# Graph layers: a ring of two groups of eight gather buffers, rows as three bf16 parts

## The reference

```python
x = x + gnn(layernorm(x), edge_index, edge_attr, ...)      # x: 6250 nodes x 256
x = x + ffn(layernorm(x), ...)                             # shared and top-2-of-8 routed experts, 256 -> 1024 -> 256

# gnn: h = x; five layers of
edge_fea = concat([edge_attr[:, 3:] @ ew1[l], edge_attr[:, 0:3] @ ew2[l]])
msg  = norm[:, None] * (h[row] + edge_fea)                 # 106250 edges; norm = dinv[row] * dinv[col]
agg  = segment_sum(msg, col)
h    = relu(concat([h, agg]) @ mlp_w[l] + mlp_b[l])
h    = batchnorm(h) * bn_g[l] + bn_b[l]                    # over the nodes; relu after it but in the last layer
```

## Time and profile before

| | us |
|---|---|
| timed runs, median | 7337.11 |
| profiled execution, first to last instruction (its span) | 8853.9 |
| preparation, to the first gather | 252 |
| gather loop of layer 0 / of layers 1 to 4 | 1480 / 1368 to 1377 |
| each of four changes of layer | 51 to 52 |
| feed-forward part | 1426 |

### The profile page before, as it was taken

How to read it: one execution, slowest core, us unless ns; L and a number is a source line. 1 busy time by engine, 2 the same in 40 slices (tenths; PEclk the granted TensorE clock), 3 DMA queues, 4 the chain that set the end, 5 groups by cost and what they waited for, 6 DMA issues and landing times. The chain is left out here.

```text
span 8853.9 us, 124916 instructions
## 1 busy us (share of the span) xinstructions
PE 6519.7 (74%) x24773; PEld 4847.4 (55%) x24774; DVE 2838.4 (32%) x9215; ACT 1624.7 (18%) x6511; POOL 4159.8 (47%) x4391
## 2 busy tenths in 40 slices
PE   3666676677777777777777777777777776789998
PEld 2444454545555545555555555555555554568886
DVE  9444444433233333333233332323222224210002
ACT  5111111111111111111121111111111112222222
POOL 0455555455555545555545555554555553210003
PEclk9777777777777777777777777777777777899999
DMA  1322222232222232222232222223222222311112
GB/s 48 90 75 73 73 73 74 76 95 79 78 78 80 78 97 80 81 77 79 79 93 83 79 77 79 81 78 96 79 79 77 79 80 74 120 51 54 54 46 85
DMA packets 316995, 687.46 MB, mean 78 GB/s; under 512 B 82064, under 2 KB 171203, under 8 KB 316819
## 3 DMA queue, kind: packets, MB, share of 16 engines
q0 software_dynamic: 214352, 590.60, 23.5%
q1 hardware_dynamic: 102594, 96.36, 3.4%
HBM read 604.38 MB, written 82.27 MB: 78 GB/s over the span
## 5 line engine op out<-in xcount | busy, mean ns | idle before, releaser
L762 POOL DMA_INDIRECT sets<-rows,index x4160 | 3951.1, 950 | 3450.0 <-ACT index L780 2213.5
L978 PE MATMUL bank<-sets 128*128 128x256 f32 (+1 forms) x8320 | 3071.7, 474 | 718.1 <-DMA sets<-rows,index 408.6
L978 PEld LDWEIGHTS bank<-sets 128*128 128x128 f32 x8320 | 1661.7, 224 | 1647.1 <-issue 954.8
L863 DVE TENSOR_SCALAR sets<-iota_row,arena,neg_base 128x128 f32<-128x128 f32 x4160 | 1470.5, 363 | 3100.7 <-PE bank L983 1295.2
L780 ACT ACTIVATE index<-arena 128x1 int32 x4160 | 789.6, 202 | 5879.7 <-PE bank L983 2184.5
L983 PE MATMUL bank<-sets 128*128 128x256 f32 (+1 forms) x3920 | 1503.1, 473 | 10.0 <-issue 9.9
L1008 PE MATMUL bank<-feat_t,mix_w 128*128 (+1 forms) x1960 | 498.0, 401 | 1201.2 <-DVE edge_sum_t L881 1168.4
L1008 PEld LDWEIGHTS bank<-feat_t,mix_w 128*128 128x128 f32 x1960 | 446.6, 296 | 1331.2 <-issue 1285.7
L983 PEld LDWEIGHTS bank<-sets 128*128 128x128 f32 x3920 | 959.5, 245 | 218.4 <-issue 19.7
L866 DVE TENSOR_SCALAR sets<-iota_row,arena,neg_base 128x128 f32<-128x128 f32 x1960 | 700.9, 358 | 0.0
L1368 PE MATMUL bank<-sets,arena 128*128 128x256 f32 x2480 | 651.1, 390 | 59.5 <-ACT arena L1384 23.1
(11 more groups left out here) (231 smaller groups left out, 2862.1 us busy)
## 6 DMA issues: line engine op xcount, KB each, us to landing
sets<-rows,index POOLq DMA_INDIRECT x4160
expert_out<-arena SPq DMA_DIRECT2D x109, 256.0 KB, 2.2
rows<-sets SPq DMA_DIRECT2D x48, 512.0 KB, 4.1
arena<-expert_in SPq DMA_DIRECT2D x54, 256.0 KB, 2.7
rows<-sets SPq DMA_DIRECT2D x12, 514.0 KB, 7.3
sets<-in_L_ffn_W1p_dram POOLq DMA_DIRECT2D x6, 1024.0 KB, 6.1
sets<-in_L_ffn_W2p_dram POOLq DMA_DIRECT2D x6, 1024.0 KB, 8.4
out_dram<-resid SPq DMA_DIRECT2D x48, 128.0 KB, 1.7
```

Source lines behind the costliest of these rows:

```text
L762: pool.indirect_dma_start(got[:, j, 0:width], None, rows0 if first else rows, bass.IndirectOffsetOnAxis(ap=index[:, j:j + 1], axis=0)).the ...
L863: ins = dve.tensor_scalar(hot[:, j, :], iota_row[:], dst_col[:, ds(c + j, 1)], neg_base[:, ds(t, 1)], ALU.subtract, ALU.is_equal)
L978: mm = pe.matmul(into(t), hot[:, j, :], got[:, j, 0:width], start=False, stop=last and j == K - 1)
```

## The change

The eight buffers become sixteen, in two groups (`R = 2`). Gathers, one-hots, matmuls and the copy of the indices are counted by group: the eight gathers of a group count on one semaphore, SP waits for all of them and counts `landed`, PE waits for `landed` and `hot_in` once a group, and counts `group_done` at its end. ACT copies eight columns of indices with one instruction, and POOL issues eight gathers after one wait. The rows in DRAM are three bf16 numbers for each value (high, middle, low, which sum to the fp32 value), 1536 bytes in place of 1024; one-hots are bf16. PE does three bf16 matmuls where it did one in fp32. The attributes of layer 0 are split in the same way (twelve columns), with one more small matmul a chunk. The split is made where rows are written: at the end of layers 0 to 3 ACT rounds to the high part (`high`), DVE subtracts, ACT rounds to the middle (`middle`), POOL subtracts for the low; `rows0` likewise, from two slots of four tiles in place of four. The loops of the layer's end are written out. `mix` moves from after chunks 2 and 4 to after 4 and 6.

```diff
+R = 2
+PARTS = 3
...
+    HW = PARTS * D
+    W0 = HW + 2
+    AP3 = PARTS * A
...
-    rows0 = nc.dram_tensor("rows0", (NP, W0), F32).ap()
-    rows = nc.dram_tensor("rows", (NP, D), F32).ap()
+    rows0 = nc.dram_tensor("rows0", (NP, W0 // 2), I32).ap()
+    rows = nc.dram_tensor("rows", (NP, HW), BF16).ap()
...
+                def high(i):
+                    if i >= 2:
+                        act.wait_ge(row0_stored[i % 2], 16 * (i // 2))
+                    for u in range(min(4, NT - i * 4)):
+                        t = i * 4 + u
+                        last = act.activation(row0_out[:, i % 2, u, 0:D], resid[:, t, :], ACT.Identity,
+                                              bias=row0_shift[:, t:t + 1], scale=row0_scale[:, t:t + 1])
+                    last.then_inc(row0_hi, 1)
+
+                def middle(i):
+                    nt = min(4, NT - i * 4)
+                    act.wait_ge(row0_rest, i + 1)
+                    act.activation(row0_out[:, i % 2, 0:nt, D:2 * D], row0_f[:, i % 2, 0:nt, :], ACT.Copy)\
+                        .then_inc(row0_mid, 1)
...
-        got = graph(K * 264).rearrange("p (j d) -> p j d", j=K)
-        hot = graph(K * P).rearrange("p (j n) -> p j n", j=K)
-        index = sb("index", [P, K], I32)
+        got = graph(R * K * GW // 2).bitcast(BF16).rearrange("p (j d) -> p j d", d=GW)
+        got_words = sets[:, 0:R * K * GW // 2].bitcast(I32).rearrange("p (j d) -> p j d", d=GW // 2)
+        hot = graph(R * K * P // 2).bitcast(BF16).rearrange("p (j n) -> p j n", n=P)
+        row_rest = graph(4 * 2 * D).rearrange("p (s t d) -> p s t d", s=4, t=2)
+        index = sb("index", [P, R * K], I32)
...
-        gathered = [sem(f"gathered{j}") for j in range(K)]
+        gathered = [sem(f"gathered{r}") for r in range(R)]
+        landed = sem("landed")
         hot_in = sem("hot_in")
-        chunk_done = sem("chunk_done")
+        attr_v = sem("attr_v")
+        group_done = sem("group_done")
...
+                    with sp.Fori(0, steps):
+                        now = sp.snap(quad, min_val=0, max_val=MAX_ALL)
+                        for r in range(R):
+                            sp.wait_ge(gathered[r], now * (16 * K) + 16 * K)
+                            sp.sem_inc(landed, 1)
+                        sp.reg_add(quad, quad, 1)
...
-                        for u in range(GG):
-                            now = pool.snap(g, min_val=0, max_val=MAX_ALL)
-                            for j in range(K):
-
-                                pool.wait_ge(index_ready, now * K + j + 1)
-                                gated(pool)
+                        now = pool.snap(quad, min_val=0, max_val=MAX_ALL)
+                        for r in range(R):
+                            pool.wait_ge(index_ready, now * R + (r + 1))
+                            gated(pool)
+                            for j in range(r * K, r * K + K):
                                 pool.indirect_dma_start(
-                                    got[:, j, 0:width], None, rows0 if first else rows,
-                                    bass.IndirectOffsetOnAxis(ap=index[:, j:j + 1], axis=0)).then_inc(gathered[j], 16)
-                            pool.reg_add(g, g, 1)
-
+                                    got_words[:, j, 0:W0 // 2] if first else got[:, j, 0:HW], None, rows0 if first else rows,
+                                    bass.IndirectOffsetOnAxis(ap=index[:, j:j + 1], axis=0)).then_inc(gathered[r], 16)
+                        pool.reg_add(quad, quad, 1)
+                    if final:
+                        return
+                    for p in range(NPAIR):
+                        w = min(2, NT - p * 2)
+                        pool.wait_ge(rows_mid, l * NPAIR + p + 1)
+                        gated(pool)
+                        into = new_rows[:, p // 2 % 4, p % 2 * 2:p % 2 * 2 + w, :]
+                        pool.tensor_tensor(into[:, :, 2 * D:HW], row_rest[:, p % 4, 0:w, :], into[:, :, D:2 * D],
+                                           ALU.subtract).then_inc(rows_lo, 1)
...
-                    for j in range(K):
-                        act.wait_ge(chunk_done, now * K + j + 1)
-                        act.activation(index[:, j:j + 1], src_col[:, ds(c + j, 1)], ACT.Copy).then_inc(index_ready, 1)
...
+                    def high(p):
+                        w = min(2, NT - p * 2)
+                        act.wait_ge(row_taken, l * NPAIR + p + 5)
+                        gated(act)
...
+                        act.activation(new_rows[:, p // 2 % 4, p % 2 * 2:p % 2 * 2 + w, 0:D], row_rest[:, p % 4, 0:w, :],
+                                       ACT.Copy).then_inc(rows_hi, 1)
+
+                    def middle(p):
+                        w = min(2, NT - p * 2)
+                        act.wait_ge(rows_rest, l * NPAIR + p + 1)
+                        gated(act)
+                        act.activation(new_rows[:, p // 2 % 4, p % 2 * 2:p % 2 * 2 + w, D:2 * D], row_rest[:, p % 4, 0:w, :],
+                                       ACT.Copy).then_inc(rows_mid, 1)
...
+                        at = now % R * K
+                        dve.wait_ge(group_done, now + 1)
+                        gated(dve)
                         for j in range(K):
-                            dve.wait_ge(chunk_done, now * K + j + 1)
-                            ins = dve.tensor_scalar(hot[:, j, :], iota_row[:], dst_col[:, ds(c + j, 1)],
+                            ins = dve.tensor_scalar(tile(hot, at + j), iota_bf, dst_col[:, ds(c + j, 1)],
                                                     neg_base[:, ds(t, 1)], ALU.subtract, ALU.is_equal)
                             if shared:
-                                ins = dve.tensor_scalar(hot_2[:, j, :], iota_row[:], dst_col[:, ds(c + j, 1)],
+                                ins = dve.tensor_scalar(tile(hot_2, at + j), iota_bf, dst_col[:, ds(c + j, 1)],
                                                         neg_base_2[:, ds(t, 1)], ALU.subtract, ALU.is_equal)
-                            if first:
-                                dve.wait_ge(gathered[j], now * 16 + 16)
-                                ins = dve.tensor_scalar(got[:, j, W0:WA], tile(attr_col, c + j),
-                                                        got[:, j, D:W0], None, ALU.mult)
-                            ins.then_inc(hot_in, 1)
+                        if first:
+                            dve.wait_ge(landed, now + 1)
+                            gated(dve)
+                            here = got[:, ds(at, K), :]
+
+                            def attr_part(n):
+                                return here[:, :, W0 + n * A:W0 + n * A + A]
+
+                            def then(n, ins):
+                                ins.then_inc(attr_v, 1)
+                                dve.wait_ge(attr_v, now * 4 + n)
+                                gated(dve)
+
+                            then(1, dve.tensor_tensor(attr_rest[:, 0, :, :], attr_col[:, ds(c, K), :],
+                                                      here[:, :, HW:W0].bitcast(F32).to_broadcast([P, K, A]), ALU.mult))
+                            then(2, dve.tensor_copy(attr_part(0), attr_rest[:, 0, :, :]))
+                            then(3, dve.tensor_tensor(attr_rest[:, 1, :, :], attr_rest[:, 0, :, :], attr_part(0),
+                                                      ALU.subtract))
+                            then(4, dve.tensor_copy(attr_part(1), attr_rest[:, 1, :, :]))
+                            ins = dve.tensor_tensor(attr_part(2), attr_rest[:, 1, :, :], attr_part(1), ALU.subtract)
+                        ins.then_inc(hot_in, 1)
...
+                    def whole(p):
+                        w = min(2, NT - p * 2)
+                        dve.wait_ge(rows_lo, l * NPAIR + p + 1)
+                        gated(dve)
+                        dve.tensor_tensor(row_rest[:, p % 4, 0:w, :], turned_pair(p, w),
+                                          dinv[:, p * 2:p * 2 + w].unsqueeze(2).to_broadcast([P, w, D]), ALU.mult)\
+                            .then_inc(row_taken, 1)
+
+                    def rest(p):
+                        w = min(2, NT - p * 2)
+                        dve.wait_ge(rows_hi, l * NPAIR + p + 1)
+                        gated(dve)
+                        dve.tensor_tensor(row_rest[:, p % 4, 0:w, :], row_rest[:, p % 4, 0:w, :],
+                                          new_rows[:, p // 2 % 4, p % 2 * 2:p % 2 * 2 + w, 0:D], ALU.subtract)\
+                            .then_inc(rows_rest, 1)
...
+                        pe.wait_ge(landed, now + 1)
+                        gated(pe)
+                        pe.wait_ge(hot_in, now + 1)
+                        gated(pe)
+
+                        def add(t, ones, j, start, stop):
+                            here = tile(got, at + j)
+                            for n in range(PARTS):
```

(59 more changed lines are left out.)

188 lines of the change are left out of this document (117 added, 71 removed).

## The result

The changed kernel takes 8440.0 us (median of 4 runs, 8432.5 to 8450.3), the kernel before 7335.2 us beside it: ratio 1.150, 95% interval 1.149 to 1.152. The forecast was 8370 us.

The account below looks back on a forecast made before the run. POOL's gather issue set the floor, 10.03 us a group; waits by group would add stops. 7337 + 887 (loops) + 150 (layer changes and preparation) = 8374, say 8370 us, 14% slower; range 7750 to 9000.

Parts of the forecast that it names:

- The chain of a last group: Gather loops: issue 8.8, landing 3.3, PE 10.6, release 1.7 us; 24.4 us a two-group tile against POOL's 20.1.
- The hop: Last gather's start to PE's first matmul: 2.9 us plus an estimated 0.4 through SP and for bytes, 3.3 us.
- D: PE's work on a tile's last group: 8.9 us at full clock, 16.4 at half, put at 10.6.
- The rate of the gather: POOL in the loops: each gather stays 0.95 us with a 0.30 us gap, despite 1536-byte rows.
- The rival of growing bytes: Gathers lengthen with their bytes to 1.43 us, a group takes 13.8 us, time 9260 us; chance 0.04.
- The port lock: DVE's bf16 one-hots shut POOL out of its descriptor port, up to 30 us a tile, 9800 us; chance 0.02.
- The gap goes with the waits: POOL's gap between gathers shrinks by 0.25 us over seven steps, 22.6 us a tile, time 7930 us; chance 0.04.
- Layer 0: Five linked attribute steps between landing and PE add 1.2 us to each of 49 tiles, 60 us (0 to 110).
- The end of the preparation: Writing rows0 with more bytes, two slots and more ACT activations adds about 18 us (5 to 40).
- Changes of layer: Splitting rows at four layer ends adds 33 us each, 132 us in all (60 to 240).
- Level of before: Loops of the kernel before, by subtraction: 7337 less 1884 us outside them, 5453 us, 10.49 us a group.
- The rivals of the clock: PE in last groups: always full clock, 7950 us, chance 0.17; or always half clock, 9790 us, chance 0.03.

Follow-up runs that it names:

- land: Changed kernel with a semaphore for each gather and PE waiting for landings chunk by chunk, release still by group; 7546.7 us, ratio 1.027.
- warm40: Changed kernel with 40 extra fp32 matmuls of 128 columns before PE's wait in a tile's last group; 8301.8 us (1.127), second chip 11482.8 us (1.294).
- run 62: Not a run: the words say that layers 1 to 4 run 62 us below 1103 us each without the wait for whole groups.
- two_rings: Layer 0 as in defer_prep, layers 1 to 4 as in ring8; 7347.0 us, ratio 0.998 to the kernel before.
- defer_prep: defer, with ACT also writing the middle part ahead of the next high part for rows0; 7347.8 us (0.998), second chip 10145.9 us (1.143).
- defer: land, with layer 0's attribute products moved behind the group's other matmuls; 10178.3 us (1.147) on the second chip.
- ring8: Changed kernel with one group of 8 buffers at fixed addresses and every wait by the chunk, bf16 parts kept; 9068.7 us (1.023), second chip.

## Why the prediction was right, step by step

- *The chain of a last group.* Right, part by part and in sum, and shown by land: with the group's landing wait gone so are the stops. The hop was mis-sized (3.9 for 3.3: SP sees the count 3.1 us after the gather's start, and PE's sequencer needs 0.8 more, register instructions for its addresses among it), as was D (10.1 for 10.6). That these two offset each other was luck.
- *The rate of the gather* held: 0.95 us and 0.30. The rival of growing bytes falls. The prediction knew nothing of the stops once in 112 gathers. An estimate by the Trainium skill, "DMA: Bandwidth & Descriptors", "Anatomy of one DMA — SWDGE (gpsimd) path", was 0.15 us a gather for the bytes in flight. The trace has 2.9 us to PE's first matmul before and 3.1 us to SP's count after; no run separates the bytes from the hop.
- *The port lock* falls: the gathers are as even beside bf16 one-hots (940 to 1190 ns) as beside fp32 ones. On the rule in the Trainium skill, "SBUF — State Buffer", "Who interferes with whom", this says little, since no run shows whether those one-hots used the shared ports.
- *The gap goes with the waits* falls: 0.30 us stays between gathers with no wait between them.
- *Layer 0* is the first mis-sized term: 1406 us, 147 more than the mean of the others, for 60. I counted 1.2 us for DVE's five linked steps in a tile; from DVE's first one to PE's first matmul it is 2.75 us on the mean, so from the last gather's start to PE's first matmul it takes 6.0 us in place of 3.9, and 16 attribute matmuls add 0.6 to D. Its 48 long stops average 7.1 us.
- *The end of the preparation* is the second: +81 us for +18. I priced bytes and ACT's activations, and missed that two slots make one chain of the step: POOL's subtraction of 1024 elements (2.06 us), the store, ACT's `high` (2.07), and `middle` (1.04) queued behind it, 9.1 us for four tiles. The earlier `middle` gave back 32 us in the timed runs of the second chip (335.5 to 300.6 us of preparation in the traces); more slots were not tried.
- *Changes of layer*: 77 to 81 us in place of 52, +108 in all for +132. POOL's subtraction was unknown; it takes 1.37 us a pair where the pairs come every 1.70 us, so it doesn't set their pace.
- *Level of before.* Its loops are still only known by subtraction. With the rest at 1363 us, as in the trace after and not 1426, they are 7335 - 252 - 206 - 1363 = 5514 us, so the loops cost +926 for +887. Here too two misses offset each other by luck: the loops after are 100 us longer than the 6340 forecast, and those before 61 us longer than I took.
- *The rivals of the clock.* Half clock is not the rule and full clock was not had; warm40 shows what it is worth. My 7950 for it was too low: with nearly all of a full-clock D the kernel takes 8302. The 16.4 us of the other rival had the three transposes still at the full clock; by its own rates it is 17.0, which changes nothing here.
- *ACT's slow register instructions belong to the profiled execution*: wrong, as far as the runs show. On the second chip the timed runs, 8861 us, are as long as that profile, and traces taken there have such instructions; those of the other two chips have none. That the profile of before came from such a chip is likely and not on record. This touched the explanation and not the number, because the level came from the timed runs.

Where the 1105 us went, from windows and the level of before above: +893 what land took away (the wait for whole groups, with most of the stops once in 112 gathers in it), +81 preparation, +83 changes of layer as in land, +300 layer 0 (1402 against 1103, a fifth of 5514), -248 for layers 1 to 4, which without that wait run 62 us below 1103 each. That is 1109. What gives the 62 us was not separated; it is not the second group of buffers, since two_rings has them too.

## What to carry to other kernels

A second group of buffers does not replace waits by the chunk: with one wait a group, landing, use and release of a whole group stand in one chain, and it is hidden only if landing, longest use and release, from the last gather's start, fit until POOL has issued the other group and could start the next (11.3 us here, 15.8 needed; the difference is about the stop). Add up that chain before merging waits. When a step's priority or its place in a queue is changed, look at what the same queue serves next: `place` behind the attribute steps seems to have taken over half of a gain.

## What was not expected of the hardware

Chips differ in how their engines' queues run. The kernel before takes 1.20 times its time on the second chip (8861 against 7348 and 7359), defer_prep 1.38 times (10146 against 7348) and warm40 1.38 times (11483 against 8302). In the traces from there single instructions come late. In defer 2310 of the 22,870 fused register instructions on PE took over 0.4 us, mostly 0.7 or 1.4 (1674 us together); in the traces of the two other chips none did.

The register instructions are not the whole of it. In warm40 on that chip only 178 of them on PE were so slow, 121 us together, and in ring8 two. Yet PE stood for "issue" 2001 us before warm40's extra matmuls, whose addresses are fixed, and 1257 us before ring8's matmuls on the gathered rows, whose buffers are at fixed addresses. So that the matmul addresses from registers are what makes a kernel suffer more, as I had expected, is not shown. What delays the instructions stays open.

A ratio measured on one chip is not that of another, and a profile has to be held against timed runs before its idle times are believed.
